# One core of Trainium2: four graph layers on 625 nodes, the second pair's shares of the last layer moved two to three items sooner and their twelve fusion products among the last items

## The reference, cut to what matters

```python
# forward: edges src -> dst, four heads of 64; backward: the same with src and dst exchanged
e = leaky_relu(a_s[src] + a_d[dst], 0.2)
alpha = softmax of e over the edges of one target
out[head] = segment_sum(alpha * h[src], dst) + bias      # heads 0..3 forward, 4..7 backward
combined = concatenate([fwd, bwd], axis=1)               # 625 x 512
fused = combined @ W_fuse + b_fuse
normed = (fused - mean) * rsqrt(var + 1e-5) * gamma + beta   # mean, var over the 625 nodes
x = x + relu(normed)
```

## Time and profile before

| | |
|---|---|
| time, median of 3 runs | 852.76 us (851.8 to 853.16) |
| profiled execution | 853.6 us, of which the span of the trace is 851.6 us |
| TensorE busy | 803.9 us (94%) |
| VectorE busy | 617.1 us (72%) |
| ScalarE busy | 456.4 us (54%) |
| GpSimd busy | 483.8 us (57%) |
| chain that ended last | TensorE 64%, VectorE 16%, GpSimd 5%, ScalarE 5% |

### The profile page before, as it was taken

The page is one execution under the profiler, slowest core; times in us unless marked ns, Lnnn a source line. Parts: engine busy times, 40 slices in busy tenths (PEclk is TensorE's granted clock), DMA queues, the critical chain, the costliest instruction groups (busy, mean ns, idle before and its releaser), DMA issues.

```text
span 851.6 us, 16365 instructions
## 1 busy us (share of the span) xinstructions
PE 803.9 (94%) x5978; PEld 708.0 (83%) x5978; DVE 617.1 (72%) x1268; ACT 456.4 (54%) x783; POOL 483.8 (57%) x542
## 2 busy tenths in 40 slices
PE   3988899999999999999999999999999999999896
PEld 2888777799998889999888999887999988875566
DVE  8899888955768664575775477677347776699996
ACT  5999673344861343583333377233438633256674
POOL 7344744584624678352666654357746339457971
PEclk9999999999999999999999999999999999989999
DMA  6000112330100143010033310014211002100121
GB/s 167 3 1 1 50 34 70 99 99 28 53 10 26 45 144 100 13 50 14 26 105 101 83 38 26 13 39 142 73 38 51 13 1 87 38 1 32 50 62 60
DMA packets 49762, 44.34 MB, mean 52 GB/s; under 512 B 6013, under 2 KB 37439, under 8 KB 49698
## 3 DMA queue, kind: packets, MB, share of 16 engines
q1 hardware_dynamic: 47234, 39.72, 16.2%
q10 hardware_dynamic: 2464, 3.80, 1.4%
HBM read 42.04 MB, written 1.33 MB: 51 GB/s over the span
## 4 chain that ended last, share of the span: by engine, by line
PE 64%; DVE 16%; POOL 5%; ACT 5%; issue 4%; SPq 3%; DMA 1%; DVEq 1%; POOLq 0%; ACTq 0%
PE psum L1858 21%; PE psum L2022 8%; PE psum L1969 8%; PE psum L1864 8%; PE psum L1888 6%; PE psum L1939 5%; POOL ringw L1457 2%; PE psum L960 2%; SPq L1274 2%; DVE arena L1038 2%; PE psum L902 1%; PE psum L2164 1%; PE psum L1912 1%; DVE stats L2529 1%; DVE acc L2637 1%
## 5 line engine op out<-in xcount | busy, mean ns | idle before, releaser
L1386 POOL TENSOR_SCALAR acc<-acc,rden,flag 128x628 f32<-128x628 f32 x80 | 69.4, 868 | 116.3 <-DVE rden L2399 116.2
L1969 PE MATMUL psum<-ringw,arena 128*128 128x512 f32 (+1 forms) x480 | 120.3, 398 | 1.5 <-DVE arena L2444 1.1
L1858 PE MATMUL psum<-arena,ringw 128*128 128x314 f32 x768 | 114.9, 310 | 0.1
L1858 PEld LDWEIGHTS psum<-arena,ringw 128*128 128x128 f32 x768 | 113.1, 190 | 1.5 <-DVE arena L2376 1.1
L1969 PEld LDWEIGHTS psum<-ringw,arena 128*128 128x128 f32 (+1 forms) x480 | 86.6, 186 | 21.8 <-DVE arena L2444 1.9
L2403 DVE TENSOR_TENSOR arena<-psum,arena 128x640 fp32r<-128x640 f32 x80 | 65.6, 820 | 35.2 <-ACT arena L1647 35.2
L1858 PE MATMUL psum<-arena 128*128 128x314 f32 (+1 forms) x480 | 88.1, 320 | 3.1 <-DVE arena L2403 1.7
L2022 PE MATMUL psum<-arena 128*128 128x384 f32 (+3 forms) x480 | 82.4, 311 | 0.0
L2376 DVE SCALAR_TENSOR_TENSOR arena<-psum,cols,arena 128x628 fp32r<-128x628 f32 x32 | 27.9, 871 | 73.7 <-ACT arena L1626 73.7
L1858 PEld LDWEIGHTS psum<-arena 128*128 128x128 f32 (+1 forms) x480 | 70.7, 187 | 6.6 <-DVE arena L2403 2.7
L1888 PE MATMUL psum<-ident,acc 128*128 128x128 f32 (+1 forms) x528 | 75.9, 272 | 0.0
(11 more groups left out here) (322 smaller groups left out, 1836.7 us busy)
## 6 DMA issues: line engine op xcount, KB each, us to landing
raw<-in_L_gnn_m_w SPq DMA_DIRECT2D x16, 256.0 KB
xn<-in_L_gnn_m_w SPq DMA_DIRECT2D x16, 256.0 KB
raw<-in_L_gnn_wv SPq DMA_DIRECT2D x8, 256.0 KB
xn<-in_L_gnn_wv SPq DMA_DIRECT2D x8, 256.0 KB
raw<-in_L_gnn_wq SPq DMA_DIRECT2D x8, 256.0 KB
xn<-in_L_gnn_wq SPq DMA_DIRECT2D x8, 256.0 KB
raw<-in_L_gnn_wk SPq DMA_DIRECT2D x8, 256.0 KB
xn<-in_L_gnn_wk SPq DMA_DIRECT2D x8, 256.0 KB
```

Of the source, the lines that this page charges most:

```text
L1386: g.tensor_scalar(pbuf[:, k % 4, 0:NW], pbuf[:, k % 4, 0:NW], rden[:, k:k + 1], flag[:, 1, k % NT:k % NT + 1], ALU.mult, ALU.mult).then_in ...
L1858: ins = pe.matmul(big[buf(u)][0:l.shape[1], h, 0:HW], l, r[:, h * HW:(h + 1) * HW], start=(i == 0), stop=(i == len(terms) - 1))
L1969: ins = pe.matmul(brow(ROWBLK[f"{name}{t}"])[0:KEYS[t], :], l, r, start=(pieces[0] + i == 0), stop=(pieces[-1] == KT - 1 and i == len(term ...
```

## The change

The second pair's steps get numbers of their own. VectorE's `inverse(1)` goes from n = 27 to 25, GpSimd's `shared(1)` from behind n = 33 to behind n = 31 (an item whose mask VectorE adds), ScalarE's `comb_high(1)` from n = 35 to 33, VectorE's `comb_rest(1)` from n = 39 to 36. TensorE does `fuse(0, pair 1)` and `fuse(1, pair 1)` behind item 36. The first pair's steps, the third pair's and SyncE's order stay.

```diff
--- before.py
+++ after.py
@@ -122,6 +122,9 @@
 TURN = list(range(L3H, NJ)) + list(range(L3H))
 PAIR = [TURN[2 * p] // 2 for p in range(NJ // 2)]
 EARLY = 3
+SHARED = [4 * NT + 3, 6 * NT + 1]
+COMB_HIGH = [5 * NT, 6 * NT + 3]
+COMB_REST = [5 * NT + 4, 7 * NT + 1]
 DVE_ADDS = [26, 28, 31, 33, 36, 38]
 
 MORE = 5 * NT
@@ -653,8 +656,8 @@
                     if n == 0:
                         g.wait_ge(misc_read, MISC["mt4"] + 1)
                     g.tensor_tensor(item(n)[:, 0:NW], item(n)[:, 0:NW], mask_of(st, TURN[i]), ALU.add).then_inc(em_up, 1)
-                if st == 3 and i in (4, 6):
-                    shared((i - 4) // 2)
+                if n in SHARED:
+                    shared(SHARED.index(n))
             shared(2)
 
             for o in range(KT):
@@ -792,8 +795,8 @@
                 for p in range(1, NJ // 2):
                     if n == 2 * NT * p - 6:
                         target_rows(p)
-                if st == 0 and i in (5, 7):
-                    comb_high((i - 5) // 2)
+                if n in COMB_HIGH:
+                    comb_high(COMB_HIGH.index(n))
             sixth_share()
             last_sums()
             comb_high(2)
@@ -974,9 +977,10 @@
                 if n == (NJ - 1) * NT:
                     pe.wait_ge(va_read, NJ - 1)
                     fuse(1, range(1))
-
-            for o in range(2):
-                fuse(o, range(1, 2))
+                if n == (NJ - 1) * NT + 1:
+                    for o in range(2):
+                        fuse(o, range(1, 2))
+
             pe.wait_ge(va_read, NJ)
             fuse(2, range(2))
             for o in range(3):
@@ -1111,12 +1115,12 @@
                     maximum(m)
                     if (m + 1) % (2 * NT) == 0:
                         targets(m // (2 * NT))
-                if st == 2 and i in (3, 5):
-                    inverse((i - 3) // 2)
+                if n in (3 * NT + 2, 5 * NT):
+                    inverse(i // 2 - 1)
                 if n == (NJ - 1) * NT + 2:
                     inverse(2)
-                if st == NT - 1 and i in (5, 7):
-                    comb_rest((i - 5) // 2)
+                if n in COMB_REST:
+                    comb_rest(COMB_REST.index(n))
             if NJ * NT - 1 in DVE_ADDS:
                 masked(NJ * NT - 1)
 
```

## The result

| | before | changed |
|---|---|---|
| median of 8 runs | 852.64 us (851.8 to 854.2) | 855.75 us (854.04 to 858.92) |
| ratio | | 1.0034, 95% interval 1.0023 to 1.0045 |

By the ratio the changed kernel is slower by 2.9 us (2.0 to 3.8); the two medians are 3.1 apart. The forecast was 2.4 more and a time of 855.2. Run again on another occasion, the changed kernel had 856.26 us beside 853.22, a ratio of 1.0032 (1.0020 to 1.0044).

What follows compares the result with a forecast made beforehand. The last item bounds the end, through copies, reciprocal, remainder and 60 products. GpSimd's 1.15 plus the twelve's 1.77 less 0.5 gave 2.4 us, from 852.76 to 855.2, with 8 in 10 from 853.6 to 857.0.

Steps and rivals of the forecast that it cites:

- What bounds the end: Behind the loop: last item, copies, reciprocal, remainder, 60 products set the end, so taking twelve products away there gains nothing.
- The twelve cost 1.3 us ahead of the last items: TensorE between items 36 and 37: twelve products take 1.77 us, less a pause taken as 0.5.
- GpSimd's wait, 1.5 us, and 1.15 at the last item: GpSimd waits 1.5 us for the shares ahead of `shared(1)`; add 35, then the last item, come 1.15 later.
- The 0.5 from one hold-up less: GpSimd's adds: one hold-up by VectorE less, a gain of 0.5 us if the shares are there at 814.3.
- The store stands behind the branch rows: SyncE's queue: the reciprocals' store stays at 808.25 behind the branch rows, so the sooner inversion brings no sooner shares.
- VectorE's stall is long and hidden: VectorE ahead of `comb_rest(1)`: stands 2.4 us, then until add 35 ends, hidden behind the late TensorE.
- The landing by the Trainium skill: DMA of the shares: 2.4 us estimated by the page for 160 KB; the forecast kept the trace's 3.3.
- The sum, 2.4 us: At the last item: 1.15 + 1.77 - 0.5 = 2.4 us later, passed on rigidly to the end.
- The clock: Rival, 11%: new TensorE pauses ahead of item 32 and the 60 products lower the clock, 1.5 us more, 856.7.

Runs made afterwards that it cites:

- x4: Kernel before with the second pair's twelve products for o = 0 and 1 left out of the computation; ratio 1.0012 to before.
- x2: Changed kernel with GpSimd's sharing of the second pair back behind item 33; ratio 1.0024 to before.
- x10: Changed kernel with SyncE's store of the second pair's reciprocals ahead of the last pair's branch rows; ratio 1.0024 to before.
- x12: The changed kernel run again, nothing altered; 856.26 us beside 853.22, ratio 1.0032 to before.
- x3: Kernel before with only GpSimd's sharing of the second pair moved ahead of add 32; ratio 1.0010 to before.
- x1: Changed kernel with the twelve products back behind the loop; ratio 1.0011 to before.
- x7: Changed kernel with twelve more products for o = 0 in the pause ahead of the last 60; ratio 1.0031 to before.
- x5: Changed kernel with twelve more products behind the loop and six more of the first pair ahead of item 32; ratio 1.0036 to before.

## Why the prediction was right

- **What bounds the end**: right. x4 leaves TensorE twelve products less and the 60 start at the same place.
- **The twelve cost 1.3 us ahead of the last items**: right, 1.13 in x2, 1.14 in x10 and 1.16 in x12. Their 1.77 fill a pause of 0.6, where 0.5 was assumed.
- **GpSimd's wait, 1.5 us, and 1.15 at the last item**: right in kind and somewhat too dear. The wait was between 0.74 and 1.99 in the six profiled executions that have it, as the landing moved. For its wait of 1.28 x12 has 0.97 at item 35. One step on the way was wrong: the prediction led the delay through adds 34 and 35, while in the changed kernel it goes from add 32 through items 32 to 34 on TensorE. The 0.5 from one hold-up less was right (adds 34 and 35 take 1.51 in x12), so add 35 ends only 0.73 later there. But the copies ahead of item 35 wait for item 34 on TensorE. In x3, where the chain does go through adds 34 and 35, add 35 is held up (2.09) and the wait of 0.74 is handed on whole.
- **The store stands behind the branch rows**: right, shown by x10.
- **VectorE's stall is long and hidden**: right, 2.13 for 2.4 us, shown by x1.
- **The landing by the Trainium skill** (DMA: Bandwidth & Descriptors, Anatomy of one DMA), an estimate of 2.4 us, was too short in every run here: the loads of the shares landed 2.9 to 4.2 us after their issue. That section is on DMAs issued by GpSimd, and these are issued by SyncE.
- **The sum, 2.4 us**: x12 has 2.13 without the clock; the measured 2.9 and 2.7 have both 2.1 and 2.4 inside their intervals. That the measured time came within 0.6 us of the forecast is partly luck: the two terms were 0.3 too dear together, and the measured values lie 0.6 to 0.8 above the 2.13 for a reason that stays open.
- **The clock** was a rival with 11%. In the profiled executions it fell among the last 60 in three (changed, x4, x10) of the five that have the pause of 1.81 us, and in none of the others, so 11% was too little. Its price was set at 1.5 in all and was 1.5 to 1.6 for one fall, 3.1 for the two of the first profile. What it adds to the median stays open: x2, x10 and x4 measure 0.8 to 1.0 above what their profiles have without the clock, which would fit. But x7 and x5, where the pauses are filled, measure 0.6 and 1.2 above theirs as well.

## What to carry to other kernels

Before products are moved out of a tail, look at what the tail waits for. If it is a chain on another engine that starts from the last item, the tail's products are covered, and moved ahead of the last item they are paid in full less one short pause. A step that is moved sooner on one engine brings nothing while the transfer behind it stands in a queue whose order is unchanged; the engine that is to use the result then waits in order, with the critical work behind it.

## What the runs showed of the hardware

TensorE paused for 1.8 us six times in the part of the last layer that is compared here: 1.84 ahead of item 32 in the changed kernel, and 1.81 ahead of the last 60 products in five kernels. Behind four of the six the granted clock was at its lower level (0.50) no later than 1.3 us after work had begun again, behind two (x2, x12) it stayed at 1.00. Behind the four pauses of 0.62 to 1.14 us ahead of item 32 (x1, x3, x7, x12) it stayed at 1.00 too. After a fall the 60 products took 10.5 in place of 8.8 to 9.0 us. That filling such pauses showed in the trace and not in the medians was not expected.
